# Re-timing the helper work of the first attention layer: weight rounding, block values, softmax sums and a bias broadcast

## The chip, the core and the metric

One core of a Trainium2 chip runs the whole program. The metric is device time in microseconds of one execution. The kernel before takes 1959.18 us (median of three runs, 1958.71 to 1961.47). Its five engines are named as in the profile: PE is TensorE (matmuls and transposes), DVE is VectorE, ACT is ScalarE, POOL is GpSimd, SP is SyncE, which here only issues DMAs. Each engine works through its own instructions in order and waits on semaphores.

## The reference, cut to what matters

The program is four layers in a row over x of 4 x 1024 tokens by 256. The change lies in the first one, a gated cross-attention to a context of 77 tokens with 16 heads of width 16:

```python
def _L0_xattn_ref(q, k, v, wq, bq, wk, bk, wv, bv, wo, bo):
    qh = (q @ wq.T + bq) ...            # 16 heads of 16
    kh = (k @ wk.T + bk) ...
    vh = (v @ wv.T + bv) ...
    attn = softmax(einsum('bhqd,bhkd->bhqk', qh * SCALE, kh))
    out = einsum('bhqk,bhkd->bhqd', attn, vh)
    return out @ wo.T + bo
x = x + tanh(g_xattn[0]) * _L0_xattn_ref(_layernorm(x), ctx, ctx, ...)
x = x + tanh(g_ffn[0]) * _L0_ffn_ref(_layernorm(x), ...)   # ternary weights
```

After it come a feed-forward layer, a second cross-attention and a self-attention, which the change does not touch.

## The kernel before, in words

`first_attention` treats the tokens in 32 tiles of 128, two tiles to a pair n, four pairs to a batch entry b. All engines run a loop over the same step number T from -12 to 34, and each engine's list of work for a step is written out by hand. In step T:

- PE does the scores of tile T+2, the transposes of the probabilities of tile T, in odd steps the transpose of the widened reciprocals of pair n-1 (`reciprocals`, L398) and the q projection of pair n+2, in even steps the transpose of x (`x_transpose`) and `out_proj` of pair n-2, and in every step one half of the product with the values (`pv`, L443) of pair n-1. `pv(n, 0)` waits for `o_out` of pair n-1, which `weigh` on DVE signals. `scores(T)` waits for `shift(T-1)` of DVE.
- DVE does, in even steps, `weigh` (values times reciprocals, L760), then in every step the row maximum (L752) and `shift` (L767) of tile T+2, then `recip_sum(T)` (L774, L775): the last reduction of the softmax sum and its reciprocal. Then come side jobs: `mantissas` (L799), which gathers the mantissa bits of a chunk of feed-forward weights, layer norm statistics, and in even steps the residual.
- ACT empties PSUM and does the exponential of tile T+2 (L562).
- POOL does `fold(T+2)`, three adds that shrink the 78 probabilities of each head to 10 partial sums (`half_sum` L622, `quarter` L624, `eighth` L628), then `widen(T)` (L637), which spreads the reciprocals for PE, in odd steps `add_bias` (L645), and its own side jobs: `block_v` (L657, five multiplies, once per batch entry), `round_chunk` (L650, a CAST of a weight chunk), and every eighth step `root` (L607 to L609, L95 to L98), a chain of 15 small instructions for the layer norm of the next batch entry; `offset` follows one step later.

The numbers behind the sums: `recip_sum(T)` waits until `fold(T)` is done, and `widen(T)` waits until `recip_sum(T)` is done. POOL runs `fold(T+2)` in step T. So in the kernel before DVE asks in step T for a fold that POOL did in step T-2.

22 chunks of feed-forward weights (128 x 1024 each) pass through four staging buffers. `CHUNK_STEPS` (L22) gives the step of each; POOL rounds it and DVE collects its mantissa bits in that step. SP loads chunk i after chunk i-4 was treated by both. After the loop the layer ends when the last pair is stored, and the feed-forward layer starts behind a barrier.

At the start POOL builds masks, waits for `root_done`, and enters the loop. In step -3 it waits for two small loads (`s_wide`: the value bias and the output bias) and spreads the value bias over 128 columns (`vb_wide`, L701), from which PE computes the product of the value bias with the output weights in step -1 (`v_bias`); DVE finishes it in step 0 (`whole_bias`).

Of the kernel before, what the change touches and what calls it, by code (L numbers as in the profile page):

```python
# [8 lines left out]
ALU = mybir.AluOpType  # L9
ACT = mybir.ActivationFunctionType  # L10
AX = mybir.AxisListType

P = 128
# [5 lines left out]
RSQRT_MAGIC = 0x5F3759DF  # L19
WCH = 1024  # L20
STAGE = 4
CHUNK_STEPS = (-5, -4, 1, 2, 3, 4, 5, 6, 9, 10, 11, 12, 13, 14, 18, 19, 20, 21, 22, 26, 27, 28)  # L22
MANTISSA = 0x7FFFFF


# [39 lines left out]
def spread(ap, dim, n):  # L65

    shape = list(ap.shape)
    shape[dim] = n
    return ap.broadcast_to(shape)
# [31 lines left out]
def first_attention(nc, ident, gates, gates_src, x_src, x_dst, ctxT, wqT, wkT, wvT, woT, bias, H, ffn, head, w_stage, tag):  # L101

    B, _, S = ctxT.shape
# [15 lines left out]
    RS = 4  # L119
# [25 lines left out]
    with semaphores(nc, tag) as sem, ExitStack() as ctx:  # L145
        def sb(name, shape, dt=F32):
            return ctx.enter_context(nc.sbuf_tensor(f"{tag}_{name}", shape, dt))
# [9 lines left out]
        kbias = sb("kbias", [P, C])  # L157
        kb_masked = sb("kb_masked", [P, C, HR])
        vbias = sb("vbias", [P, C])
        vb_wide = sb("vb_wide", [P, C, P])  # L160
        obias = sb("obias", [P, D])
        kt = sb("kt", [P, 2, C, HR, S])
# [14 lines left out]
        prob_all = sb("prob", [P, PR, KC * P])  # L177
        half_sum = sb("half_sum", [P, H, HALF])
        quarter = sb("quarter", [P, H, HALF // 2])
        eighth = sb("eighth", [P, 3, H, HALF // 4])  # L180
        negmax = sb("negmax", [P, H])
        rsum = sb("rsum", [P, RS, H])
        r_wide = sb("r_wide", [P, RS, H, dh])
# [45 lines left out]
        def _(sp):  # L229
# [63 lines left out]
            store_v(0)  # L293
            for i in range(2, STAGE):
                load_chunk(i)
            for dst, src in ((vbias[:, :], bv),
                             (obias[:, :], spread(bo.rearrange("(a n) -> a n", a=1), 0, P))):
                sp.dma_start(dst, src).then_inc(s_wide, 16)
            load_w(3, wo, woT)
            load_x(PB + 2)  # L300
            load_x(PB + 3)
# [298 lines left out]
        def _(pool):  # L600
# [17 lines left out]
            def fold(T):  # L618
                pool.wait_ge(a_exp, T + 1)
                if T:  # L620
                    pool.wait_ge(p_eighth, T)
                own.step(pool.tensor_tensor(half_sum[:, :, 0:S2 // 2], prob[:, T % PR, :, 0:S2 // 2],  # L622
                                            prob[:, T % PR, :, S2 // 2:S2], ALU.add))
                own.step(pool.tensor_tensor(quarter[:, :, :], half_sum[:, :, 0:HALF // 2],  # L624
                                            half_sum[:, :, HALF // 2:HALF], ALU.add))
                if T >= 3:
                    pool.wait_ge(d_r, T - 2)
                pool.tensor_tensor(eighth[:, T % 3, :, :], quarter[:, :, 0:HALF // 4],  # L628
                                   quarter[:, :, HALF // 4:HALF // 2], ALU.add).then_inc(p_eighth, 1)

            def widen(T):
# [20 lines left out]
            def block_v(b):  # L652
                pool.wait_ge(v_in, 32 * (b + 1))
                if b >= 2:
                    pool.wait_ge(e_pv, PB * (b - 1))
                for i, k, n in runs:
                    ins = pool.tensor_tensor(v_blk[:, b % 2, i:i + n, :, :], spread(v_k[:, k:k + n, :].unsqueeze(2), 2, HR),  # L657
                                             spread(v_mask[:, i:i + n, :].unsqueeze(3), 3, dh), ALU.mult)
                ins.then_inc(v_placed, 1)
# [16 lines left out]
            for i, (_, m, k) in enumerate(tiles):  # L676
                own.link(pool.affine_select(out=v_mask[:, i, :], in_=v_mask[:, i, :], compare_op=ALU.is_ge, fill=0.0,
                                            base=S - 1 - P * k + SEG * m, pattern=[[S2, HR]], channel_multiplier=-1))
            own.wait()
            pool.wait_ge(s_pad, 1)  # L680
            pool.wait_ge(root_done, 1)
            for T in STEPS:
                n, odd = divmod(T, 2)
                if T % 8 == 0 and 1 <= (T + 8) // 8 <= B:
                    root((T + 8) // 8)
                if T % 8 == 1 and 1 <= (T + 8) // 8 <= B:
                    offset((T + 8) // 8)
                if 0 <= T + 2 < TILES:
                    fold(T + 2)
                if 0 <= T < TILES:  # L690
                    widen(T)
                if odd and 0 <= n < NP:
                    add_bias(n)
                if (T + 2) % 8 == 0 and 0 <= (T + 2) // 8 < B:
                    block_v((T + 2) // 8)
                if T in CHUNK_AT:
                    round_chunk(CHUNK_AT[T])
                if T == -3:
                    pool.wait_ge(s_wide, 32)
                    for c in range(C):  # L700
                        ins = pool.tensor_copy(vb_wide[:, c, :], spread(vbias[:, c:c + 1], 1, P))  # L701
                    ins.then_inc(s_vb, 1)

        @block.vector
        def _(dve):
# [64 lines left out]
            def recip_sum(T):  # L770
                dve.wait_ge(p_eighth, T + 1)
                if T >= RS:
                    dve.wait_ge(p_wide, T - RS + 1)
                own.step(dve.tensor_reduce(rsum[:, T % RS, :], eighth[:, T % 3, :, :], AX.X, ALU.add))  # L774
                dve.reciprocal(rsum[:, T % RS, :], rsum[:, T % RS, :]).then_inc(d_r, 1)  # L775

            def whole_bias():
# [46 lines left out]
            for T in STEPS:  # L824
                n, odd = divmod(T, 2)
                if not odd and 0 <= n - 2 < NP:
                    weigh(n - 2)
                if 0 <= T + 2 < TILES:
                    row_max(T + 2)
                if 0 <= T + 2 < TILES:  # L830
                    shift(T + 2)
                if T == 0:
                    whole_bias()
                if 0 <= T < TILES:
                    recip_sum(T)
                if T in CHUNK_AT:
                    mantissas(CHUNK_AT[T])
                if T == CHUNK_STEPS[-1] + 1:
                    mantissa_found()
                b, p = divmod(T + 12, 8)  # L840
                if p < PB and 0 <= PB * b + p < NP + HEAD:
                    ln_stats(PB * b + p)
                if not odd and 0 <= n - 2 < NP:
                    residual(n - 2)
                if T == TILES:
                    judge()
# [1906 lines left out]
def laid_out(inputs):  # L2753

    import numpy as np

    def cols(v):
        return v.reshape(-1, P).T

    a = {}  # L2760
    for name, v in inputs.items():
        v = np.asarray(v)
        if name == "x":
            a[name] = v.reshape(-1, v.shape[-1])
        elif name == "ctx_1024":
            a["ctxT"] = v.transpose(0, 2, 1)
        elif name.startswith("L0_xattn_w") or (name.startswith("L0_ffn_") and name.endswith("_w")):
            a[name + "T"] = v.T
        elif name.endswith("Wkv"):
            half = v.shape[1] // 2  # L2770
            a[name[:-3] + "Wk"], a[name[:-3] + "Wv"] = v[:, :half], v[:, half:]
        elif name in ("L0_xattn_bq", "L0_xattn_bk", "L0_xattn_bv", "L1_xattn_ln_scale", "L1_xattn_ln_bias", "L0_ffn_w1_s",
                      "L0_ffn_w2_s", "L0_ffn_h1_s", "L0_ffn_h2_s"):
            a[name] = cols(v)
        else:
            a[name] = v
    return {name: np.ascontiguousarray(v) for name, v in a.items()}
# [14 lines left out]
```

## Time and profile before

| what | value |
|---|---|
| median of three runs | 1959.18 us |
| the profiled execution's own time | 1958.71 us |
| its span | 1957.0 us |
| mean granted clock | 0.985 |
| busy over the span: PE, DVE, ACT, POOL | 94%, 61%, 55%, 37% |
| the first attention layer | about 0 to 236 us of the span |

The granted clock is a share of TensorE's full speed. The shares over the whole span say little here, since the change touches only the first 236 us: there POOL is busy nearly throughout, while it has little to do in the layer behind. "Idle before" in a row is how long the engine stood before that instruction, and the name after the arrow is what ended the wait.

### The profile page before, as it was taken

What the parts mean: (1) busy time and instruction counts of PE and PEld (TensorE: products, weight loads), DVE (VectorE), ACT (ScalarE), POOL (GpSimd) and SP (SyncE); (2) the same over time, 40 slices, a digit from 0 to 9 for tenths busy, and PEclk for the clock granted to TensorE, in tenths of its full rate; (3) what the DMA queues carried; (4) which work ended last, traced back from release to release, by engine and by line L of the source; (5) the groups of instructions that cost most, each with busy time, mean ns of one, the idle gap of its engine ahead of it and who ended that gap; (6) DMA issues with size and microseconds to landing.
All of it is one profiled execution on the core that took longest, in us unless ns stands there. A gap on an engine that the chain in (4) does not pass through costs nothing. (4 is left out here: it accounts for less than half of the span.)

```text
span 1957.0 us, 60621 instructions
## 1 busy us (share of the span) xinstructions
PE 1836.1 (94%) x26589; PEld 1491.1 (76%) x26589; DVE 1190.7 (61%) x1658; ACT 1085.4 (55%) x1900; POOL 732.3 (37%) x1008
## 2 busy tenths in 40 slices
PE   6999799999999999998899988999999999999996
PEld 4666578788887888886787867788787877887875
DVE  7888533332423323242655536888988898888885
ACT  4666444443434434342545544777777777877763
POOL 6899600000010000010433322556556565656552
PEclk9999999999999999999899998999999999999999
DMA  5332100000000000010111115212332143123211
GB/s 160 101 114 69 40 10 22 1 22 1 22 12 11 22 1 22 1 66 27 53 41 33 35 39 131 73 58 62 110 96 58 57 115 96 52 68 110 75 52 35
DMA packets 147006, 106.24 MB, mean 54 GB/s; under 512 B 19993, under 2 KB 143153, under 8 KB 146737
## 3 DMA queue, kind: packets, MB, share of 16 engines
q1 hardware_dynamic: 146736, 102.28, 17.8%
q8 instruction: 215, 3.52, 0.8%
q14 instruction: 55, 0.44, 0.1%
HBM read 76.77 MB, written 25.49 MB: 52 GB/s over the span
## 5 line engine op out<-in xcount | busy, mean ns | idle before, releaser
L2251 ACT ACTIVATE E_prob<-E_ps_s,E_negmax 128x1024 f32<-128x1024 f32 x256 | 284.9, 1115 | 143.2 <-DVE E_negmax L2564 142.8
L2564 DVE TENSOR_REDUCE E_negmax<-E_ps_s 128x1 f32<-128x1024 f32 x256 | 301.5, 1219 | 82.2 <-PE E_ps_s L2070 81.8
L2571 DVE STREAM_TRANSPOSE E_prob<-E_prob 128x1024 f32<-128x1024 f32 x256 | 303.9, 1225 | 23.9 <-ACT E_prob L2251 11.5
L2089 PEld LDWEIGHTS E_ps_o<-E_prob,E_vrep 32*64 32x64 f32 x15872 | 231.5, 130 | 63.4 <-ACT head L2277 56.9
L2089 PE MATMUL E_ps_o<-E_prob,E_vrep 32*64 32x128 f32 x15872 | 262.5, 274 | 11.6 <-ACT head L2277 3.6
L1675 ACT ACTIVATE F_raw<-F_ps,ffn_scales 128x512 f32<-128x512 f32 x128 | 88.3, 690 | 287.9 <-PE F_ps L1578 287.9
L1578 PE MATMUL F_ps<-F_ha,ffn_w_rounded 128*128 128x512 f32 x1024 | 240.7, 395 | 0.0
L1578 PE MATMUL F_ps<-F_hb,ffn_w_rounded 128*128 128x512 f32 x1024 | 240.2, 395 | 0.0
L1578 PEld LDWEIGHTS F_ps<-F_ha,ffn_w_rounded 128*128 128x128 f32 x1024 | 191.1, 188 | 48.3 <-issue 1.6
L1578 PEld LDWEIGHTS F_ps<-F_hb,ffn_w_rounded 128*128 128x128 f32 x1024 | 192.1, 188 | 46.8
L2469 POOL TENSOR_TENSOR head<-head 128x512 f32<-128x512 f32 x93 | 119.3, 1283 | 248.4 <-ACT head L2277 248.4
L1766 DVE TENSOR_TENSOR F_ha<-F_raw,F_ha 128x512 fp32r<-128x512 f32 x64 | 44.3, 693 | 184.2 <-ACT F_ha L1677 184.2
L1766 DVE TENSOR_TENSOR F_hb<-F_raw,F_hb 128x512 fp32r<-128x512 f32 x64 | 44.3, 693 | 169.2 <-ACT F_hb L1677 169.2
L95 POOL TENSOR_TENSOR F_rs<-F_rs 128x4 f32<-128x4 f32 x24 | 4.8, 199 | 352.6 <-DVE F_rs L1725 351.3
L1578 PE MATMUL F_ps<-F_xt_part,ffn_w_rounded 128*128 128x512 f32 x512 | 123.8, 400 | 8.2 <-DVE F_raw L1756 4.2
L2070 PE MATMUL E_ps_s<-E_k_hi,E_q_hi 64*128 64x512 f32 x512 | 114.5, 442 | 15.0 <-ACT E_prob L2251 13.4
L1578 PEld LDWEIGHTS F_ps<-F_xt_part,ffn_w_rounded 128*128 128x128 f32 x512 | 94.1, 190 | 35.7 <-DVE F_raw L1756 9.0
L1696 POOL TENSOR_TENSOR F_xt_part<-F_xt,F_xt_part 128x1024 fp32r<-128x1024 f32 x7 | 16.9, 2409 | 252.1 <-ACT F_xt_part L1637 144.1
L2070 PE MATMUL E_ps_s<-E_k_hi,E_q_lo 64*128 64x512 f32 x512 | 102.3, 392 | 0.0
L2070 PE MATMUL E_ps_s<-E_k_lo,E_q_hi 64*128 64x512 f32 x512 | 101.3, 390 | 0.0
L2070 PEld LDWEIGHTS E_ps_s<-E_k_hi,E_q_hi 64*128 64x128 f32 x512 | 48.0, 184 | 42.6 <-ACT E_prob L2251 23.4
L1756 DVE SCALAR_TENSOR_TENSOR F_raw<-F_ps,ffn_scales,F_silu 128x512 f32<-128x512 f32 x64 | 47.7, 750 | 53.8 <-ACT F_silu L1659 53.8
(318 smaller groups left out, 3913.3 us busy)
## 6 DMA issues: line engine op xcount, KB each, us to landing
E_vrep<-E_v_all SPq DMA_DIRECT2D x128, 256.0 KB, 3.1
shared<-in_L_ffn_h_wT SPq DMA_DIRECT2D x16, 512.0 KB, 3.9
E_v_all<-E_vst SPq DMA_DIRECT2D x32, 256.0 KB, 2.3
C_x<-x SPq DMA_DIRECT2D x20, 256.0 KB, 4.2
F_x<-x SPq DMA_DIRECT2D x9, 512.0 KB, 3.7
A_x<-in_x SPq DMA_DIRECT2D x16, 256.0 KB, 5.1
x<-A_x SPq DMA_DIRECT2D x16, 256.0 KB, 2.2
x<-F_x SPq DMA_DIRECT2D x16, 256.0 KB, 2.1
```

The source lines that it names most:

```text
L95: own.step(eng.tensor_tensor(t, y, y, ALU.mult))
L1578: mm = pe.matmul(out, fw.chunk(w, name, k, j * P, (j + 1) * P), a[:, k, :], start=k == 0 and i == 0, stop=k == K - 1 and i == len(parts) - 1)
L1675: act.activation(raw[:, u % 2, :], ps[:, u % 4, :], ACT.Gelu, scale=scale).then_inc(u_raw, 1)
L1696: pool.tensor_tensor(xt_part[1][:, :, :], xt[:, :, :], xt_part[0][:, :, :], ALU.subtract).then_inc(xt_lo, 1)
L1756: dve.scalar_tensor_tensor(out=dst, in0=ps[:, 2 * (j % 2) + 1, :], scalar=scales[:, 1, j:j + 1], in1=silu[:, j % 2, :], op0=ALU.mult, op1= ...
L1766: dve.tensor_tensor(dst, raw[:, u % 2, :], hi, ALU.subtract).then_inc(u_lo, 1)
L2070: mm = pe.matmul(ps_s[:, j, keys], a[rows, c % 2, cols], k[rows, c % 2, keys], start=i == 0, stop=i == 2)
L2089: mm = pe.matmul(low[64 * j:64 * j + 64, g, :], vrep[rows, slot, KB // 4 * (quarter % 2) + k, dh * j:dh * (j + 1)], prob[rows, u % 2, :, j ...
L2251: act.activation(prob[:, s // UT % 2, s % UT, j, :], ps_s[:, j, :], ACT.Exp, bias=negmax[:, at:at + 1], scale=1.0, accum_out=den[:, 2 * c ...
L2469: pool.tensor_tensor(part[:, 0, :], part[:, 0, :], part[:, 1, :], ALU.add).then_inc(part_added, 1)
L2564: dve.tensor_reduce(negmax[:, at:at + 1], ps_s[:, j, :], AX.X, ALU.max, negate=True).then_inc(d_max, 1)
L2571: dve.transpose(at, at).then_inc(d_t, 1)
```

## The change: what it does

Five edits, all in the first attention layer.

1. `CHUNK_STEPS` gets other numbers: two chunks move ahead of step 0 (to -2 and -1), and the others are spread to steps that reach to 27. Before: -5, -4, 1 to 6, 9 to 14, 18 to 22, 26 to 28.
2. `block_v` moves one step later, from steps 6, 14, 22 (and -2) to steps 7, 15, 23 (and -1).
3. DVE calls `recip_sum(T+1)` in step T and not `recip_sum(T)`; `eighth` has two buffers and not three.
4. The value bias is loaded as 256 single numbers from a plain vector (before: 128 runs of two numbers that lay side by side), is spread by a multiply with a tile of ones, and this is done ahead of POOL's loop: the wait for `s_wide` stands in front of everything that POOL does in the loop.
5. `whole_bias` moves on DVE from step 0 to the end of step -1.

```diff
-CHUNK_STEPS = (-5, -4, 1, 2, 3, 4, 5, 6, 9, 10, 11, 12, 13, 14, 18, 19, 20, 21, 22, 26, 27, 28)
+CHUNK_STEPS = (-5, -4, -2, -1, 1, 3, 4, 5, 6, 7, 9, 11, 12, 13, 15, 17, 19, 20, 21, 23, 25, 27)
...
-        eighth = sb("eighth", [P, 3, H, HALF // 4])
+        eighth = sb("eighth", [P, 2, H, HALF // 4])
...
-            for dst, src in ((vbias[:, :], bv),
+            for dst, src in ((vbias[:, :], bv.rearrange("(c p) -> p c", p=P)),
                              (obias[:, :], spread(bo.rearrange("(a n) -> a n", a=1), 0, P))):
-                sp.dma_start(dst, src).then_inc(s_wide, 16)
+                sp.dma_start(dst, src, allow_slow_non_contiguous=True).then_inc(s_wide, 16)
...
-                if T >= 3:
-                    pool.wait_ge(d_r, T - 2)
-                pool.tensor_tensor(eighth[:, T % 3, :, :], quarter[:, :, 0:HALF // 4],
+                if T >= 2:
+                    pool.wait_ge(d_r, T - 1)
+                pool.tensor_tensor(eighth[:, T % 2, :, :], quarter[:, :, 0:HALF // 4],
...
             own.wait()
+            own.step(pool.memset(ones[:, :], 1.0))
+            pool.wait_ge(s_wide, 32)
+            for c in range(C):
+                ins = pool.tensor_tensor(vb_wide[:, c, :], ones[:, :], spread(vbias[:, c:c + 1], 1, P), ALU.mult)
+            ins.then_inc(s_vb, 1)
             pool.wait_ge(s_pad, 1)
             pool.wait_ge(root_done, 1)
             for T in STEPS:
...
-                if (T + 2) % 8 == 0 and 0 <= (T + 2) // 8 < B:
-                    block_v((T + 2) // 8)
+                if (T + 1) % 8 == 0 and 0 <= (T + 1) // 8 < B:
+                    block_v((T + 1) // 8)
                 if T in CHUNK_AT:
                     round_chunk(CHUNK_AT[T])
-                if T == -3:
-                    pool.wait_ge(s_wide, 32)
-                    for c in range(C):
-                        ins = pool.tensor_copy(vb_wide[:, c, :], spread(vbias[:, c:c + 1], 1, P))
-                    ins.then_inc(s_vb, 1)
...
-                own.step(dve.tensor_reduce(rsum[:, T % RS, :], eighth[:, T % 3, :, :], AX.X, ALU.add))
+                own.step(dve.tensor_reduce(rsum[:, T % RS, :], eighth[:, T % 2, :, :], AX.X, ALU.add))
...
-                if T == 0:
-                    whole_bias()
-                if 0 <= T < TILES:
-                    recip_sum(T)
+                if 0 <= T + 1 < TILES:
+                    recip_sum(T + 1)
...
+                if T == -1:
+                    whole_bias()
```

Where it moves instructions. On POOL between steps 6 and 8 of the kernel before, ahead of the second `root` (which begins with L607, A_rs from A_mv); A_v_blk is `block_v`, the CAST is `round_chunk`, A_half_sum to A_eighth is one fold, A_r_wide is `widen`, A_x is `add_bias`:

```order
L657 TENSOR_TENSOR A_v_blk<-A_v_k,A_v_mask 128x96
L657 TENSOR_TENSOR A_v_blk<-A_v_k,A_v_mask 128x32
L650 CAST ffn_w_rounded<-shared 128x1024
L622 TENSOR_TENSOR A_half_sum<-A_prob 128x16x39
L624 TENSOR_TENSOR A_quarter<-A_half_sum 128x320
L628 TENSOR_TENSOR A_eighth<-A_quarter 128x160
L637 COPY A_r_wide<-A_rsum 128x128 x2
L645 TENSOR_TENSOR A_x<-A_x,A_obias 128x512
L607 TENSOR_SCALAR A_rs<-A_mv 128x8
```

The same place on POOL in the changed kernel, whose line numbers are one higher:

```order
L651 CAST ffn_w_rounded<-shared 128x1024
L623 TENSOR_TENSOR A_half_sum<-A_prob 128x16x39
L625 TENSOR_TENSOR A_quarter<-A_half_sum 128x320
L629 TENSOR_TENSOR A_eighth<-A_quarter 128x160
L638 COPY A_r_wide<-A_rsum 128x128 x2
L646 TENSOR_TENSOR A_x<-A_x,A_obias 128x512
L658 TENSOR_TENSOR A_v_blk<-A_v_k,A_v_mask 128x160
L658 TENSOR_TENSOR A_v_blk<-A_v_k,A_v_mask 128x96
L658 TENSOR_TENSOR A_v_blk<-A_v_k,A_v_mask 128x160
L658 TENSOR_TENSOR A_v_blk<-A_v_k,A_v_mask 128x96
L658 TENSOR_TENSOR A_v_blk<-A_v_k,A_v_mask 128x32
L651 CAST ffn_w_rounded<-shared 128x1024
```

`block_v` stood ahead of the fold of tile 9 and stands behind it now, and a second CAST stands between that fold and the `root`.

On DVE at the end of step 9 and the start of step 10 the names alone don't show what moved, since `recip_sum` reads alike for every tile. In the changed kernel:

```order
L753 TENSOR_REDUCE A_negmax<-A_ps_s 128x16
L768 TENSOR_TENSOR A_prob<-A_ps_s,A_negmax 128x16x77
L775 TENSOR_REDUCE A_rsum<-A_eighth 128x16
L776 RECIPROCAL A_rsum<-A_rsum 128x16
L800 TENSOR_TENSOR A_w_bits<-A_w_bits,shared 128x1024
L761 TENSOR_TENSOR A_o<-A_ps_o,A_r_t 128x512
```

The rows are those of before, but the reduction of A_eighth is that of tile 10 and not of tile 9, and behind it in the queue stand the mantissas (A_w_bits) and `weigh` (A_o) of pair 3.

## Rows read from the trace of the kernel before

**Rows 1.** Busy time by stretch: us, busy (instructions), then granted clock, DMA share, GB/s
```profile
30.00:232.00 202.00, 183.92 (x1718) 130.23 (x1717) 161.76 (x219) 126.09 (x229) 177.93 (x276) 0.97 0.25 73
```
**Rows 2.** Same view, PE alone, around four waits
```profile
45.00:56.00 11.00, 8.47 (x47) 0.69 0.16 49
99.00:107.00 8.00, 5.76 (x36) 0.79 0.35 116
150.00:158.00 8.00, 6.35 (x62) 1.00 0.10 33
```
**Rows 3.** Timeline of PE at the second root: start us, us, instruction, idle before
```profile
94.46 1.50 PE L443 MATMUL A_ps_o<-A_pt,A_v_blk 128*32 128x256 f32 x18
...
101.44 0.79 PE L398 MATMUL A_ps_m<-ident,A_r_wide 128*128 128x128 f32 x4 [2.23 <-POOL A_r_wide L637]
```
**Rows 4.** Timeline of POOL, 80 to 101 us
```profile
80.37 1.70 POOL L657 TENSOR_TENSOR A_v_blk<-A_v_k,A_v_mask 128x160 f32<-128x160 f32 x5
82.01 1.04 POOL L650 CAST ffn_w_rounded<-shared 128x1024 fp32r<-128x1024 f32 x1
...
87.83 0.24 POOL L607 TENSOR_SCALAR A_rs<-A_mv 128x8 f32<-128x8 f32 x1
...
90.82 1.01 POOL L98 TENSOR_TENSOR A_rs<-A_rs 128x8 f32<-128x8 f32 x1
...
92.79 0.20 POOL L98 TENSOR_TENSOR A_rs<-A_rs 128x8 f32<-128x8 f32 x1
...
95.64 0.49 POOL L628 TENSOR_TENSOR A_eighth<-A_quarter 128x160 f32<-128x160 f32 x1
...
100.86 0.53 POOL L637 COPY A_r_wide<-A_rsum 128x128 f32<-128x128 f32 x2
```
**Rows 5.** Timeline of ACT: the exponential of tile 9
```profile
80.36 1.23 ACT L562 ACTIVATE A_prob<-A_prob 128x1232 f32<-128x1232 f32 x1
```
**Rows 6.** Timeline of DVE, steps 9 and 10
```profile
90.10 0.31 DVE L774 TENSOR_REDUCE A_rsum<-A_eighth 128x16 f32<-128x160 f32 x1
...
90.61 1.16 DVE L799 TENSOR_TENSOR A_w_bits<-A_w_bits,shared 128x1024 int32<-128x1024 int32 x1
92.08 0.69 DVE L760 TENSOR_TENSOR A_o<-A_ps_o,A_r_t 128x512 f32<-128x512 f32 x1 [0.31 <-PE A_ps_o L443]
92.82 1.44 DVE L752 TENSOR_REDUCE A_negmax<-A_ps_s 128x16 f32<-128x1232 f32 x1
94.30 1.44 DVE L767 TENSOR_TENSOR A_prob<-A_ps_s,A_negmax 128x1232 f32<-128x1232 f32 x1
```
**Rows 7.** Timeline of PE at the first, third and fourth root
```profile
44.05 0.81 PE L412 MATMUL A_ps_s<-A_kt,A_q 32*128 32x154 f32 x16
...
47.97 1.12 PE L398 MATMUL A_ps_m<-ident,A_r_wide 128*128 128x128 f32 x4 [2.53 <-POOL A_r_wide L637]
...
146.61 1.50 PE L443 MATMUL A_ps_o<-A_pt,A_v_blk 128*32 128x256 f32 x18
...
152.86 0.66 PE L398 MATMUL A_ps_m<-ident,A_r_wide 128*128 128x128 f32 x4 [1.50 <-POOL A_r_wide L637]
...
197.20 1.50 PE L443 MATMUL A_ps_o<-A_pt,A_v_blk 128*32 128x256 f32 x18
...
202.73 0.66 PE L398 MATMUL A_ps_m<-ident,A_r_wide 128*128 128x128 f32 x4 [0.78 <-POOL A_r_wide L637]
```
**Rows 8.** Timeline of POOL: last fold instruction behind the first, third, fourth root
```profile
42.15 0.49 POOL L628 TENSOR_TENSOR A_eighth<-A_quarter 128x160 f32<-128x160 f32 x1
...
146.89 0.49 POOL L628 TENSOR_TENSOR A_eighth<-A_quarter 128x160 f32<-128x160 f32 x1
...
196.90 0.49 POOL L628 TENSOR_TENSOR A_eighth<-A_quarter 128x160 f32<-128x160 f32 x1
```
**Rows 9.** Timeline of POOL at the start
```profile
21.80 0.53 POOL L701 COPY A_vb_wide<-A_vbias 128x128 f32<-128x128 f32 x2 [2.37 <-DMA A_obias<-in_L_xattn_bo]
24.98 1.51 POOL L622 TENSOR_TENSOR A_half_sum<-A_prob 128x624 f32<-128x624 f32 x1 [2.64 <-ACT A_prob L562]
```

More of the change, by code:

```diff
@@ L159, in first_attention @@
         vbias = sb("vbias", [P, C])
+        ones = sb("ones", [P, P])
         vb_wide = sb("vb_wide", [P, C, P])
@@ L2771, in laid_out @@
             a[name[:-3] + "Wk"], a[name[:-3] + "Wv"] = v[:, :half], v[:, half:]
-        elif name in ("L0_xattn_bq", "L0_xattn_bk", "L0_xattn_bv", "L1_xattn_ln_scale", "L1_xattn_ln_bias", "L0_ffn_w1_s",
+        elif name in ("L0_xattn_bq", "L0_xattn_bk", "L1_xattn_ln_scale", "L1_xattn_ln_bias", "L0_ffn_w1_s",
                       "L0_ffn_w2_s", "L0_ffn_h1_s", "L0_ffn_h2_s"):
```

## The prediction

> **What bounds the kernel now.** I first read the busy time by stretch. From 30 to 232 us, the loop of the first attention layer, POOL is busy 177.93 of 202 us, PE 183.92, DVE 161.76 [rows 1]. Three engines run near their limit, so a wait on one soon becomes a wait on another. Then I read the timeline of PE. The two-tile period is dense, except at four places, all the same: PE stands at the transpose of the widened reciprocals and is released by POOL, for 2.53, 2.23, 1.50 and 0.78 us, 7.0 us together [rows 3, 7]. They come in steps 3, 11, 19 and 27, three steps behind a `root`. The POOL timeline gives the reason. At the second root POOL starts the chain of small instructions at 87.83, ends it at 92.99, ends the fold of tile 10 at 96.13 and starts the `widen` for which PE waits at 100.86 [rows 4]. POOL never stands still in between. These waits also cost clock: the granted clock is 0.69 and 0.79 of full speed in the stretches around the first two and 1.00 around the third [rows 2]. Of 11 and 8 us that is 3.4 and 1.7 us of full-speed time.
>
> So the layer is PE's pace plus four hold-ups by POOL, one behind each root. Of each edit I ask what it does there.
>
> **Edit 2 and 1, POOL ahead of a root.** Before, the order is `block_v`, CAST, fold of tile 9, `widen`, `add_bias`, root. Now one CAST, fold, `widen`, `add_bias`, `block_v`, CAST, root. The 1.70 us of `block_v` and one CAST of 1.04 us [rows 4] now lie behind the fold: 2.74 us more between fold and root. The fold can't move ahead by as much. The CAST ahead of it ended at 83.05, and the exponential it needs at 81.59 [rows 4, 5]: at most 1.46 us is gained. So the root starts about 1.3 us later. I take 1.3 us for roots 2, 3 and 4 (bounds 0, if the fold moves by all of it, and 2.74 us, if it doesn't move). Ahead of the first root the folds wait for their exponentials, as that of tile 0 did for 2.64 us [rows 9], so no fold can move ahead there, and `block_v` leaves a place where POOL had time to spare: there I take the full 2.74 us.
>
> **Edit 3, the reciprocal sum one step early.** This is the large term. Nothing waits for `recip_sum`: no hold-up of PE or POOL ends on it. What the edit adds is a wait. In step 9 DVE now asks for the fold of tile 10, which POOL runs in step 8 behind the root. DVE comes to this place at 90.10 [rows 6]; the fold ends at 96.13 [rows 4], with the 1.3 us at 97.4. DVE stands about 7 us. Behind it in the queue are the reciprocal, the mantissas, `weigh` of pair 3, the row maximum and the shift of tile 12. `weigh` is what `pv(4, 0)` on PE waits for, and that wait is new.
>
> The sum for the second root: 97.4, plus 0.1 for the signal, plus 0.51 (from 90.10 to 90.61) for reduction and reciprocal, plus 1.16 for the mantissas and 0.69 for `weigh` [rows 6]: 99.9 us. `pv` started at 94.46 before [rows 3], so PE is held 5.4 us. From `pv` to the transpose of the reciprocals PE took 4.75 us (94.46 to 99.21, which is 101.44 less the wait of 2.23) [rows 3]. It arrives there at 104.6; POOL has the `widen` ready at 100.86 + 0.53 + 1.3 = 102.7 [rows 4], so the old wait is gone, but PE is 3.2 us later than its 101.44. The new wait takes the place of the old one and is longer.
>
> Third root: the fold ends at 146.89 + 0.49 + 1.3 = 148.7 [rows 8], plus the same 2.5 us (in step 17 there is now a chunk too) gives 151.2 for `pv`, 4.6 us after 146.61. PE was ready at the transpose at 151.36; now 155.9, against 152.86: 3.1 us [rows 7]. Fourth root: 196.90 + 0.49 + 1.3 + 2.5 = 201.2, 4.0 us after 197.20; ready at 201.95 + 4.0 = 205.9, against 202.73: 3.2 us [rows 7, 8].
>
> First root: the fold of tile 2 ends at 42.64 + 2.74 = 45.4 [rows 8]. DVE goes on with 0.1 + 0.51 + 1.16 us, then the row maximum and shift of tile 4 at 1.44 us each [rows 6]: 50.0. The scores of tile 5 wait for that shift and started at 44.05 before: 6.0 us of wait. PE was ready for the transpose at 45.44, now at 51.4, against 47.97: 3.5 us [rows 7].
>
> Together 3.5 + 3.2 + 3.1 + 3.2 = 13.0 us. The clock: idles of 2.53 and 2.23 us were followed by the lower clock, that of 1.50 was not [rows 2, 3, 7]. By those rows the third and fourth root now pay it too, with idles of 4 to 4.6 us. I take 1.7 us each, the smaller of the two prices in rows 2 (bounds 0 and 3.4): 3.4 us. The lower clock at roots 1 and 2 stays as it is.
>
> **What the moved chunks give.** Two chunks leave the loop behind step 0: two CASTs of 1.04 us and two mantissa instructions. Those drop out at steps where POOL later waits for an exponential, so PE gains nothing: 0. Bound: the two CASTs and one further us each on POOL, 4 us. That further us is seen in the trace: the mantissa instruction runs on DVE from 90.61, and a POOL instruction of 128x8 issued at 90.82 took 1.01 us where its like at 92.79 took 0.20 [rows 4, 6]. The Trainium skill says why (SBUF — State Buffer, section Who interferes with whom): a DVE instruction with two SBUF inputs shares a port with a POOL instruction that reads SBUF, and the later one waits. The trace agrees. By that rule alone the change would be a gain, with fewer such meetings in the loop; it is the rival "relief" below.
>
> **Edit 4, the start.** POOL waits for both bias loads at the front of the loop. Before, it rounded two chunks and then waited 2.37 us, until 21.80 [rows 9]. Now the chunks come after: 21.80 + 0.53 + two CASTs of 1.04 = 24.4. The first fold waits for an exponential and started at 24.98: hidden. If each meets a mantissa instruction and takes 1 us more, some 1.5 us shows. What stands behind: SP holds chunk 4 until chunk 0 is rounded, and behind chunk 4 in its queue are the loads of the values that `block_v` needs. Both CASTs had ended by 19.43 before (21.80 less the wait) and end at 24.4 now, so these loads come 5 us later; `block_v` itself comes later too, behind one more fold. I take 0, bound 4 us. The Trainium skill (DMA: Bandwidth & Descriptors, section Why small descriptors are slow) would have the load of 256 single numbers slower; the wait ended on the other load, that of the output bias [rows 9], so it changes nothing here until it lands behind that.
>
> **Edit 5** moves two short DVE instructions that PE needs only for the first `pv` from one step to the end of the step before: 0.
>
> **Sum.** 1958.71 us of the profiled execution + 13.0 + 3.4 = 1975.1 us. That execution lies 0.5 us under the median of 1959.18. I predict 1975.
>
> **The rivals.**
> - *Held by the late root alone* (slower, smaller). DVE has room to catch up, so its wait doesn't reach PE, and only the later start of the roots is paid: 2.7 + 3 x 1.3 = 6.6 us, 1965 us. For it: DVE is the least busy of the three, 161.76 of 202 us [rows 1]. Against: `weigh` lies directly behind the wait and `pv` needs it at once. It decides if `weigh` is ready within 2 us of PE's coming.
> - *Relief* (faster). The chunks, not the roots, made POOL late. If fewer meetings per period bring each `widen` ahead of PE, the 7.0 us of waits and the 5.1 us of clock go: 1947 us at best; with only the two chunks of POOL work saved, 4 us, 1955. It decides from the point at which the folds behind a root end before DVE asks, some 6 us earlier than in rows 4 and 6. Nothing in the rows moves them by so much.
> - *Late start.* The sum above, and in addition the values come late for `block_v`: up to 4 us more, 1979.
> - *No effect*: the waits move, and PE's own work fills the time; 1957 to 1961. Against it: PE does nothing while it waits in order.
>
> **How the numbers follow.** Forecast 0.66, late root alone 0.13, late start 0.06, no effect 0.08, relief 0.07. A measurement of this kernel tells 0.2%, 3.9 us, from no change. Slower: 0.66 + 0.13 + 0.06 less 0.01 for the low edge = 0.84; same 0.09; faster 0.07. The range goes down to 1963 (1.3 us per root turned to 0 takes 3.9, the clock price 3.4, a part of DVE's wait absorbed the rest), which takes in rival one, and up to 1982 (clock at 3.4 us per root adds 3.4, roots 2.74 us late add 4.3, less what overlaps). The likeliest case alone: 1969 to 1981.
>
> **What would show it.** In the changed profile: DVE waits at the reduction of A_eighth, released by POOL's `eighth`, four times for some 5 to 7 us, where the whole layer had almost none. PE waits at `pv` for DVE's A_o three times for 4 to 5 us, once at the scores for DVE's A_prob, and its wait for A_r_wide is gone. The granted clock drops below 1.00 behind all four roots. The feed-forward layer starts some 16 us later, and all behind it is as long as before. I am wrong if the wait of DVE is short or absent, if POOL's root starts no later against PE, or if PE's waits in the loop add up to no more than before.

## The result and the profile after

| what | before | after |
|---|---|---|
| median of the timed runs, us | 1960.33 (1958.71 to 1961.95, 4 runs) | 1981.03 (1979.26 to 1983.30, 4 runs) |
| the profiled execution's own time, us | 1958.71 | 1977.79 |
| its span, us, and mean granted clock | 1957.0, 0.985 | 1976.1, 0.981 |
| first layer, until the feed-forward layer's first transpose | 241.5 us | 253.8 us |
| the rest of the span | 1715.5 us | 1722.3 us |

The ratio is 1.0101 [1.0082, 1.012]: slower by 1%. A later comparison of the same two kernels gave 1.0086 [1.007, 1.0101], 1976.94 against 1961.16 us. The profiled execution and one more of the kernel after took 1977.79 and 1975.92 us. By the two ratios the change costs some 17 to 20 us (the medians differ by 20.7 and 15.8). Of the 19.1 us between the two profiled spans, 12.3 lie in the first layer and 6.8 behind it, where not one instruction differs; the last experiment asks which of them the change caused.

The first view is the list of waits between 30 and 255 us of the kernel after: who waits for whom, then us in total, how many times, the longest. Here, too, the line numbers of the kernel after are one higher than those of the kernel before.

```profile
DVE A_rsum L775 <- POOL A_eighth L629: 29.7, 13, 6.4
POOL A_half_sum L623 <- ACT A_prob L563: 28.1, 14, 3.2
...
PE A_ps_o L444 <- issue: 13.0, 3, 4.4
...
PE A_ps_s L413 <- DVE A_prob L768: 5.5, 2, 4.9
...
PE A_ps_m L399 <- POOL A_r_wide L638: 0.5, 1, 0.5
```

The same view of the kernel before, from the same stretch:

```profile
POOL A_half_sum L622 <- ACT A_prob L562: 9.4, 6, 3.2
...
PE A_ps_m L398 <- POOL A_r_wide L637: 7.0, 4, 2.5
...
DVE A_rsum L774 <- POOL A_eighth L628: 0.4, 1, 0.4
```

PE's 7.0 us behind the widened reciprocals are down to 0.5. In their place stand 13.0 us in three waits at `pv` and 4.9 at the scores, and DVE waits 29.7 us for POOL's fold where it waited 0.4; 22.2 us of them are four waits, one behind each root. POOL itself stands idle for longer than before, 28.1 us against 9.4, and still every root holds PE up: what counts is when POOL is late, not how busy it is.

PE in the kernel after (start us, duration us, engine, instruction, idle before), at the second root, where it answers to [rows 3], and at the third and fourth:

```profile
99.43 2.76 PE L444 MATMUL A_ps_o<-A_pt,A_v_blk 128*32 128x256 f32 x18 [4.22 <-issue]
...
105.65 0.60 PE L399 MATMUL A_ps_m<-ident,A_r_wide 128*128 128x128 f32 x4
...
153.82 2.55 PE L444 MATMUL A_ps_o<-A_pt,A_v_blk 128*32 128x256 f32 x18 [4.42 <-issue]
...
208.19 2.31 PE L444 MATMUL A_ps_o<-A_pt,A_v_blk 128*32 128x256 f32 x18 [4.40 <-issue]
```

The transpose of the reciprocals no longer waits, but comes at 105.65 and not at 101.44. The idle time stands at `pv`, all three times, and the profile calls its end "issue": it found no releaser. DVE's rows name it. The first four are those of the start, for later; the others are the second root and answer to [rows 6]:

```profile
28.68 1.50 DVE L800 TENSOR_TENSOR A_w_bits<-A_w_bits,shared 128x1024 int32<-128x1024 int32 x1
...
31.44 0.40 DVE L782 TENSOR_TENSOR A_obias<-A_ps_o,A_obias 128x256 f32<-128x256 f32 x1
31.87 0.78 DVE L783 TENSOR_SCALAR A_obias<-A_obias,gates 128x256 f32<-128x256 f32 x1
...
34.03 1.44 DVE L768 TENSOR_TENSOR A_prob<-A_ps_s,A_negmax 128x1232 f32<-128x1232 f32 x1
...
89.39 1.44 DVE L768 TENSOR_TENSOR A_prob<-A_ps_s,A_negmax 128x1232 f32<-128x1232 f32 x1
97.05 0.32 DVE L775 TENSOR_REDUCE A_rsum<-A_eighth 128x16 f32<-128x160 f32 x1 [6.21 <-POOL A_eighth L629]
...
97.57 1.16 DVE L800 TENSOR_TENSOR A_w_bits<-A_w_bits,shared 128x1024 int32<-128x1024 int32 x1
98.65 0.68 DVE L761 TENSOR_TENSOR A_o<-A_ps_o,A_r_t 128x512 f32<-128x512 f32 x1
```

`weigh` ends at 99.33 and `pv` starts at 99.43. It waits in the code for just that. POOL, which answers to [rows 4]:

```profile
82.13 1.52 POOL L623 TENSOR_TENSOR A_half_sum<-A_prob 128x624 f32<-128x624 f32 x1 [1.57 <-ACT A_prob L563]
...
86.82 1.69 POOL L658 TENSOR_TENSOR A_v_blk<-A_v_k,A_v_mask 128x160 f32<-128x160 f32 x5
88.45 1.04 POOL L651 CAST ffn_w_rounded<-shared 128x1024 fp32r<-128x1024 f32 x1
89.58 0.24 POOL L608 TENSOR_SCALAR A_rs<-A_mv 128x8 f32<-128x8 f32 x1
...
96.53 0.48 POOL L629 TENSOR_TENSOR A_eighth<-A_quarter 128x160 f32<-128x160 f32 x1
```

The root starts 1.75 us later, at 89.58 instead of 87.83, but the fold that DVE waits for ends only 0.88 us later, at 97.01 instead of 96.13. The root itself got shorter: its slow instruction of 1.01 us in [rows 4] met the mantissas on DVE. Now DVE stands still while the root runs, its mantissas come at 97.57, and every instruction of the root takes 0.20 to 0.25 us.

PE's clock, in the columns of [rows 2]: behind the wait at the scores, at the first root, and in the stretches ahead of the third and fourth reciprocal transposes.

```profile
34.00:42.00 8.00, 6.38 (x34) 0.57 0.20 68
45.00:56.00 11.00, 9.79 (x95) 1.00 0.14 49
...
153.00:161.00 8.00, 7.18 (x55) 0.79 0.06 18
208.00:216.00 8.00, 7.74 (x57) 0.79 0.11 35
```

Last, the layer cut at the four transposes of the reciprocals behind a root: stretch, its length, PE's busy time (instructions), granted clock, DMA share, GB/s. Before:

```profile
0.00:47.97 47.97, 29.83 (x204) 0.99 0.54 163
47.97:101.44 53.47, 50.20 (x452) 0.94 0.34 101
101.44:152.86 51.42, 49.10 (x453) 0.97 0.34 104
152.86:202.73 49.87, 47.65 (x453) 1.00 0.22 64
202.73:241.50 38.77, 28.07 (x254) 0.96 0.10 33
```

After:

```profile
0.00:49.11 49.11, 29.70 (x205) 0.90 0.60 181
49.11:105.65 56.54, 49.42 (x454) 0.97 0.31 87
105.65:160.04 54.39, 49.14 (x454) 0.97 0.31 93
160.04:214.41 54.37, 49.14 (x454) 0.97 0.18 53
214.41:253.80 39.39, 28.11 (x256) 0.99 0.10 34
```

The five lengths grow by 1.1, 3.1, 3.0, 4.5 and 0.6 us. In the fourth row, length less busy time is PE's idle time, 2.22 us before and 5.23 after, and the clock goes from 1.00 to 0.97, which is 1.6 us of 54.37: 3.0 + 1.6 = 4.6 us, against the measured 4.5.

The first length, 1.1 us, understates the change. The two executions did not enter the loop at the same time: PE starts the scores of tile 2 at 30.37 us before and at 28.14 after, and kernels with the same code up to there start them anywhere from 28.3 to 30.4 us (before, once more, e1, e7, e9). Counted from the scores of tile 2, the first length is 17.60 us before and 20.97 after, so it grows by 3.4 us, and the whole layer by 14.5. Of these, 11.1 are idle time of PE and 3.4 are busy time, which is what the lower clock makes of the same work.

### The profile page after: what moved, and what is told of

It is laid out like the page before. It is cut to its first block and busy times, and to the rows that moved or that the text cites. A ratio compares the mean times of both kernels' runs of the same rounds, so it can differ in the third digit from the quotient of the medians.

```text
span 1976.1 us, 60623 instructions
## 1 busy us (share of the span) xinstructions
PE 1841.2 (93%) x26589; PEld 1493.8 (76%) x26589; DVE 1188.5 (60%) x1658; ACT 1083.7 (55%) x1900; POOL 723.0 (37%) x1009
```

## The experiments

Each kernel was profiled, and timed beside the kernel before on the same chip. "Layer" is the time until the feed-forward layer's first transpose in the profiled execution (before 241.5, after 253.8).

**The reciprocal sum alone, and all but it.** `e1_recip_only` is the kernel before with edit 3 alone:

```diff
-                if 0 <= T < TILES:
-                    recip_sum(T)
+                if 0 <= T + 1 < TILES:
+                    recip_sum(T + 1)
```

> The kernel before with edit 3 alone: the reciprocal sum of tile T+1 in step T, and two eighth buffers. Theory (DVE is held by the fold behind the root): at the second root the fold ends at 96.1 as before, then 0.1 + 0.51 + 1.16 + 0.69 us, pv at 98.6 instead of 94.46, the transpose of the reciprocals at 103.3 instead of 101.44; third and fourth root without a chunk behind the wait, 0.6 us each; first root 0.7 us. Together some 4 us, 6 with a lower clock after two of the waits; DVE waits for eighth about 5 us behind each root. Rival (only the late root costs, DVE's wait is absorbed): 0 us, because the root starts where it did.

Measured: 1969.25 us, ratio 1.0043 [1.003, 1.0055], 8.4 us; layer 245.7. `e2_all_but_recip` is the kernel after with that one edit undone (the value bias spread by a copy, with no tile of ones).

> The changed kernel with edit 3 undone: recip_sum(T) in step T and three eighth buffers. The value bias is spread by a copy as in the kernel before, still at the front of the loop, since the tile of ones has no room beside the third buffer. Theory: DVE's long waits and PE's waits at pv go, PE waits again for the widened reciprocals, a little longer than before, since the roots start 1.3 us late: 3 to 6 us over the kernel before, 14 to 17 us under the changed one. Rival (late root or chunks are the main cost): at least 12 us over the kernel before.

Measured: 1965.9 us, ratio 1.003 [1.0018, 1.0042], 5.9 us; layer 244.3. The two halves, 8.4 and 5.9, make 14.3 of the change's 17 to 20 us: they nearly add up. DVE at the second root in `e1_recip_only`:

```profile
92.36 0.32 DVE L774 TENSOR_REDUCE A_rsum<-A_eighth 128x16 f32<-128x160 f32 x1 [3.86 <-POOL A_eighth L628]
...
93.96 0.68 DVE L760 TENSOR_TENSOR A_o<-A_ps_o,A_r_t 128x512 f32<-128x512 f32 x1
```

and PE there:

```profile
94.74 1.50 PE L443 MATMUL A_ps_o<-A_pt,A_v_blk 128*32 128x256 f32 x18 [1.89 <-issue]
...
100.71 0.63 PE L398 MATMUL A_ps_m<-ident,A_r_wide 128*128 128x128 f32 x4 [1.23 <-DVE A_x L788]
```

The wait is edit 3's: it is there with none of the rest. But at the second root it is 3.86 us and not 6.21, and `pv` is held 1.89 us and not 4.22. The other 2.3 us come with the late root. The 8.4 us are more than the 4 to 6 expected. A term that nobody had counted is DVE's residual: PE waits for it 9.0 us in nine waits, against 1.8 us in three before. In `e2_all_but_recip` DVE waits 6.5 us for the fold and not 29.7, and PE's old wait is longer than in [rows 3]:

```profile
100.69 0.66 PE L398 MATMUL A_ps_m<-ident,A_r_wide 128*128 128x128 f32 x4 [3.41 <-POOL A_r_wide L637]
```

Its four such waits sum to 9.5 us (7.0 before). So each half of the change costs by itself, and both do so behind the same roots.

**The later block values alone.** `e3_blockv_only`, the kernel before with edit 2:

```diff
-                if (T + 2) % 8 == 0 and 0 <= (T + 2) // 8 < B:
-                    block_v((T + 2) // 8)
+                if (T + 1) % 8 == 0 and 0 <= (T + 1) // 8 < B:
+                    block_v((T + 1) // 8)
```

> The kernel before with edit 2 alone: block_v one step later. Theory: the 1.70 us of block_v stand between fold and root, of which up to 1.4 us come back, since the fold ahead can start earlier: 0.3 to 1.7 us per root in PE's wait for the widened reciprocals, 1 to 5 us in all. Rival (block_v's place does not matter): 0 us.

Measured: 1970.43 us (1959.96 to 1976.95), ratio 1.0044 [1.0011, 1.0076]; layer 246.8. The interval is wide, from 2 to 15 us; that it costs something is shown, how much is not. PE's four waits for A_r_wide sum to 9.9 us, 2.9 more than before. Behind the third, of 1.71 us, the granted clock is 0.79 from 154 to 162 us, where [rows 2] have 1.00 behind a wait of 1.50. So in this execution the late root cost clock beside its wait; whether the longer wait brought it stays open, as the last section shows.

**The chunks alone.** `e4_chunks_only`, the kernel before with edit 1:

```diff
-CHUNK_STEPS = (-5, -4, 1, 2, 3, 4, 5, 6, 9, 10, 11, 12, 13, 14, 18, 19, 20, 21, 22, 26, 27, 28)
+CHUNK_STEPS = (-5, -4, -2, -1, 1, 3, 4, 5, 6, 7, 9, 11, 12, 13, 15, 17, 19, 20, 21, 23, 25, 27)
```

> The kernel before with edit 1 alone: the new steps of the chunks. Theory: a CAST of 1.04 us comes right in front of the roots 2 to 4, and one behind the fold of tile 1: about 1 us per root later, 2 to 4 us slower in all. Rival (relief, fewer meetings of mantissas and POOL instructions in the loop): 4 us faster.

Measured: 1964.65 us, ratio 1.0021 [1.001, 1.0032]; layer 241.8. The waits for A_r_wide are 3.43 us at the first root and 3.38 at the second, and the four sum to 10.1 us, 3.1 more than before. That is as expected: two chunks fewer in the loop did not help, and the chunks at steps 7, 15 and 23, between fold and root, are the likely cost. `e8_before_new_chunks` asked for the gain alone: one chunk leaves the loop to step -2, others leave steps 5, 14 and 21 for 25 and 29, and none is put in front of a root:

```diff
-CHUNK_STEPS = (-5, -4, 1, 2, 3, 4, 5, 6, 9, 10, 11, 12, 13, 14, 18, 19, 20, 21, 22, 26, 27, 28)
+CHUNK_STEPS = (-5, -4, -2, 1, 2, 3, 4, 6, 9, 10, 11, 12, 13, 18, 19, 20, 22, 25, 26, 27, 28, 29)
```

> The kernel before with other chunk steps, chosen so that fewer CASTs lie between POOL's last wait for an exponential and the widen behind a root: (-5, -4, -2, 1, 2, 3, 4, 6, 9, 10, 11, 12, 13, 18, 19, 20, 22, 25, 26, 27, 28, 29); the chunks of steps 5, 14 and 21 are taken out. Theory: PE's waits behind roots 2 to 4 of 2.23, 1.50 and 0.78 us shrink by about 1 us each, and the lower clock behind the second goes: 3 to 6 us faster than before. Rival (the number of chunks in the loop matters, not their place): 1 us or nothing.

Measured: 1961.77 us, ratio 1.0006 [0.9995, 1.0018]. No gain, no loss, where 3 to 6 us had been expected. The wait at the second root fell only from 2.23 to 1.51 us, at the first it stayed at 2.54, at the fourth it rose from 0.78 to 1.51, and a new one of 2.10 us came near the end of the loop. The five waits sum to 8.1 us, against 7.0: other chunk steps moved the waits and did not shorten their sum.

**The bias alone.** `e5_bias_only`, the kernel before with edit 4 (the loads as single numbers, the wait ahead of the loop, the spread by a copy):

```diff
-            for dst, src in ((vbias[:, :], bv),
+            for dst, src in ((vbias[:, :], bv.rearrange("(c p) -> p c", p=P)),
...
+            pool.wait_ge(s_wide, 32)
+            for c in range(C):
+                ins = pool.tensor_copy(vb_wide[:, c, :], spread(vbias[:, c:c + 1], 1, P))
+            ins.then_inc(s_vb, 1)
...
-                if T == -3:
-                    pool.wait_ge(s_wide, 32)
```

> The kernel before with edit 4 alone (bias loaded as single numbers, spread at the front of POOL's loop; by a copy, since the tile of ones has no room). Theory: hidden by the exponential of tile 0, 0 us, at most 1. Rival (late start: the queue of SP behind the first CAST brings the values late for block_v): up to 4 us slower.

Measured: 1959.8 us, ratio 0.9991 [0.9978, 1.0005]: nothing. POOL's rows at the start:

```profile
22.56 0.53 POOL L682 COPY A_vb_wide<-A_vbias 128x128 f32<-128x128 f32 x2 [15.45 <-DMA A_obias<-in_L_xattn_bo]
...
25.02 1.50 POOL L622 TENSOR_TENSOR A_half_sum<-A_prob 128x624 f32<-128x624 f32 x1
```

POOL stands for 15.45 us, and its first fold starts at 25.02, where [rows 9] have 24.98. The wait still ends on the load of the output bias, not on that of the 256 single numbers, so what these cost does not show.

**A shorter root.** If the roots are what holds everything up, a shorter root must give time back in both kernels. These two leave out two of the three Newton steps of the `root` inside the loop, 8 of its 15 instructions:

```diff
-                newton(own, pool, half, y, t)
+                newton(own, pool, half, y, t, 1)
```

> The changed kernel with one Newton step instead of three in POOL's root (two thirds of the iteration left out, for the layer norms of batch entries 1 to 3 and the two pairs behind them). One Newton step takes 1.17 us on POOL (90.49 to 91.67 in the changed kernel), so each root is 2.3 us shorter. Theory: DVE's wait of 6.2 to 6.4 us behind each root and PE's wait of 4.2 to 4.4 us at pv shrink by 2.3 us each, and the lower clock behind them shrinks or goes: 7 to 12 us faster than the changed kernel. Rival (the roots are not what holds DVE): less than 2 us.

> The kernel before with the same short root. Theory: PE's four waits for the widened reciprocals, 7.0 us, shrink by up to 2.3 us each and nearly go, 6.8 us, and with them most of the 5.1 us of lower clock: 6 to 11 us faster than before. Rival (PE's own work fills the time): 0 us.

Measured: on the kernel after 1966.1 us, 1.0024 [1.0007, 1.004] of before; layer 241.8, 12.0 us less than after. On the kernel before 1950.53 us, 0.9949 [0.9932, 0.9966], which is 10 us faster; layer 229.4, 12.1 us less. The prediction had put down 7.0 us of waits and 5.1 of clock for the roots, together just these 12.1; but against the second profile of before, with its layer of 238.7 us, the gain is 9.3. So it is 9 to 12 us, and the roots hold both kernels up. Both gain alike: with the short root the change still costs 12 to 15 us. PE at the second root in `e7_before_short_root` has neither the wait nor the low clock that followed it in [rows 2]:

```profile
93.44 0.66 PE L398 MATMUL A_ps_m<-ident,A_r_wide 128*128 128x128 f32 x4
...
94.88 1.96 PE L383 MATMUL A_ps_m<-A_xt,A_wq 128*128 128x256 f32 x8
```

In `e6_after_short_root` PE stands at `pv` for 1.93, 2.11 and 2.11 us, in place of 4.22, 4.42 and 4.40:

```profile
95.33 1.50 PE L444 MATMUL A_ps_o<-A_pt,A_v_blk 128*32 128x256 f32 x18 [1.93 <-issue]
```

**The root on another engine.** The same question without leaving anything out: `e9_before_root_on_dve` (and `e10_after_root_on_dve`) take `root` and `offset` from POOL's loop and let DVE do them ahead of its residual:

```diff
-                if T % 8 == 0 and 1 <= (T + 8) // 8 <= B:
-                    root((T + 8) // 8)
-                if T % 8 == 1 and 1 <= (T + 8) // 8 <= B:
-                    offset((T + 8) // 8)
...
+                if T % 8 == 0 and 1 <= (T + 8) // 8 <= B:
+                    b = (T + 8) // 8
+                    dve.wait_ge(stat, b)
+                    whole_root(mv[:, b % 2, :, :], rs[:, b % 2, :, :]).then_inc(root_done, 1)
```

> The kernel before with the roots of batch entries 1 to 4 computed by DVE (the chain it already runs for entry 0, 2.5 us from 13.51 to 15.97) behind the mantissas of steps 0, 8, 16 and 24, and none on POOL. At those steps 8, 16 and 24 DVE stood 1.67 us waiting for the out projection. Theory (POOL's root is what makes the widen late): PE's four waits of 7.0 us go, and 5 us of lower clock with them, less about 1 us per root for a later residual: 8 to 12 us faster than before. Rival (the work only moves to DVE, which is as full): 0 us, or slower.

> The changed kernel with the same move of the roots to DVE. Theory (the edits cost time only because the root stands in front of the fold that DVE now asks for early): DVE's waits of over 6 us for eighth and PE's waits of over 4 us at pv go, and the time comes to within 4 us of the kernel before with this move: 25 us or more under the changed kernel. Rival (the edits cost something of their own): it stays 8 us or more above the kernel before with this move.

Measured: 1969.97 us, 1.0056 [1.0038, 1.0074], on the kernel before; 1976.82 us, 1.0087 [1.0069, 1.0106], on the kernel after. What was expected of POOL came: the waits for A_r_wide are gone, and POOL stands idle 35.8 us in `e9_before_root_on_dve`. The time did not follow, since DVE became late instead. DVE at the second root there:

```profile
84.65 1.20 DVE L710 TENSOR_TENSOR A_rs<-A_rs 128x8 f32<-128x8 f32 x1
85.89 1.43 DVE L711 TENSOR_TENSOR A_rs<-A_rs 128x8 f32<-128x8 f32 x1
87.35 0.17 DVE L712 SCALAR_TENSOR_TENSOR A_rs<-A_rs 128x8 f32<-128x8 f32 x1
...
89.62 0.75 DVE L784 SCALAR_TENSOR_TENSOR A_x<-A_ps_m,gates,A_x 128x512 f32<-128x512 f32 x1
```

and PE:

```profile
90.52 1.09 PE L398 MATMUL A_ps_m<-ident,A_r_wide 128*128 128x128 f32 x4 [3.37 <-DVE A_x L784]
```

The chain took 5.5 us (84.10 to 89.62), and PE waits for the residual behind it. The 8 to 12 us faster that had been expected did not come; the rival, that the work only moves to DVE, did. The experiment shows that POOL's lateness and PE's old wait hang together. It does not show what a free root would be worth; the short root comes nearer to that.

The second of the two comes out level with the kernel after, where 25 us less had been expected, and 6 to 7 us above the first, between what the theory allowed (4) and what the rival said (8). With no root on POOL, DVE's waits for the fold sum to 9.0 us and not to 29.7, and PE no longer stands at `pv` for 4 us. By this, most of what the five edits cost, 17 to 20 us, hangs on the root in front of the fold. But DVE is late here for a reason of its own, so the 6 to 7 us are no clean measure of the rest.

**The rest of the program.** `c2_after_again` and `c1_before_again` are the two kernels once more, unchanged.

> The changed kernel once more, beside the kernel before on the same chip. In the profiled executions the first layer accounts for 12.3 us of 19.1 and the layers behind it for 6.8 us, though their instructions are the same. Theory A (the rest is the difference of single executions in TensorE's clock): the first layer is again 12 us longer than before, the rest differs by another amount, and the medians differ by less than 19 us. Theory B (the layers behind really get slower): 19 to 21 us again.

> The kernel before once more, for a second profile. Theory A: the time from the start of the feed-forward layer to the end, 1715.5 us in the first profile, is some us longer in this one, without any cause in the code. Theory B: it is 1715.5 within 1 us.

Measured: 1976.94 us (6 runs) for the kernel after, layer 255.3, rest 1720.4. For the kernel before one execution of 1963.42 us, layer 238.7, rest 1723.0. So theory A holds. The rest of the span in all profiled executions, where all fourteen run the same code: before 1715.5, after 1722.3, and in the order of the experiments (e1 to e10) 1717.6, 1719.9, 1725.5, 1724.0, 1718.3, 1722.9, 1717.5, 1720.8, 1718.1, 1719.0. The kernel before holds both the lowest value and, once more, one above that of after. So the 6.8 us behind the layer are scatter between executions. The layer is longer by 12.3 us in the first pair of profiles, by 16.6 in the second. Counted from the scores of tile 2 it is 14.5 and 17.8.

The second profile of before holds a surprise. PE waits at the first two roots as in [rows 3, 7], even a little longer, but the granted clock behind both waits stays at 1.00, where [rows 2] have 0.69 and 0.79:

```profile
47.06 0.66 PE L398 MATMUL A_ps_m<-ident,A_r_wide 128*128 128x128 f32 x4 [2.81 <-POOL A_r_wide L637]
...
98.31 0.66 PE L398 MATMUL A_ps_m<-ident,A_r_wide 128*128 128x128 f32 x4 [2.53 <-POOL A_r_wide L637]
```

```profile
45.00:56.00 11.00, 7.98 (x70) 1.00 0.17 54
98.00:106.00 8.00, 7.54 (x66) 1.00 0.23 74
```

## Why the prediction was right, step by step

- *What bounds the kernel*: right in the waits. A shorter root takes 9 to 12 us out of the layer of before, where waits and clock were put at 7.0 + 5.1. The clock is the weak half of this: the same waits came without the 5.1 us in the second profile of before. The view by stretch had said only that three engines are nearly full; the four waits in PE's timeline said where.
- *Edit 3, the wait added*: right in place and size for roots two to four. DVE's waits at the four roots were 3.22, 6.21, 6.39 and 6.37 us (about 7 forecast for the second), and `pv` was held 4.22, 4.42 and 4.40 (5.4, 4.6, 4.0). The term 3.2 + 3.1 + 3.2 is one of waits; PE's idle time grew by 3.9, 2.9 and 3.0 us in these three stretches, and by 3.4, 2.6 and 3.1 in the second pair of profiles.
- *First root*: the size came, by another path. It was put at 3.5 us; counted from the scores of tile 2 the stretch grew by 3.4 us, and by 3.7 in the second pair. But the working had PE held for 6.0 us at the scores of tile 5, behind DVE's long wait. DVE's wait for the fold was only 3.22 us, and these scores waited 0.66. PE was held 4.88 us two tiles earlier, at the scores of tile 3, where it had waited 1.34 before. Its idle time in the stretch grew by 0.8 us, as its old waits went; the other 2.6 us are slower work, at a clock of 0.57 from 34 to 42 us. That the sum fits is luck. Why DVE was late at tile 3: in its rows at the start the mantissas of a moved chunk (28.68, 1.50 us) and `whole_bias` (31.44 to 32.65; edit 5) lie ahead of the row maximum and of the shift that PE waits for (34.03), though PE had done the scores of tile 2 at 28.95. The kernels with edit 5 wait 3.9 to 5.5 us at those scores (after, once more, e2, e6, e10), the nine profiles without it 1.3 to 1.4. All with edit 5 have edits 1, 2 and 4 too, and edits 1, 2 and 4 one by one leave the wait at 1.35. So edit 5, put at 0, was perhaps not free, alone or together with edit 1; its own two instructions take 1.2 us. No run has it alone, and its share stays open.
- *The late root*: forecast 1.3 us, 1.75 seen at the second (87.83 to 89.58). The fold ahead of it started 0.9 us sooner. Of the 1.75 us only 0.88 reached the fold behind the root, since the root no longer meets the mantissas: here the rival "relief" had a true part, of 0.8 us. The rival that charged the late roots alone said 6.6 us. `e2_all_but_recip`, which is nearly that case, cost 5.9, of which the waits for A_r_wide are 2.5 and the longer wait at the scores of tile 3 is 2.8.
- *Clock*: right in size in the first pair, for a reason that does not hold. Between 30 and 232 us the full-speed time lost (one less the granted clock, added up over windows of 2 us) rose from 5.1 to 8.5 us, by the 3.4 forecast. The two prices of 1.7 us at the third and fourth root came: 0.79 over 8 us. At the second root the price stayed. At the first it moved: 1.00 from 45 to 56 us, where [rows 2] have 0.69, and 0.57 from 34 to 42 us instead. At the 1.2 GHz level `pv` at the second root took 2.76 us, at 2.4 GHz 1.50. In the second pair the same sum rose from 1.7 to 12.0 us. So "the lower clock at roots 1 and 2 stays as it is" and the fixed 1.7 us per root were lucky: the clock behind like waits differs from execution to execution.
- *Moved chunks and start*: 0 forecast for both. Edit 4 by itself cost nothing. Edit 1 cost 4.1 us by itself where it had been counted only as part of the late root.
- *The sum*: 13.0 + 3.4 = 16.4 us. Counted from the scores of tile 2, the layer grew by 11.1 us of idle and 3.4 of busy time in the first pair, by 11.9 and 5.9 in the second: 14.5 and 17.8. The medians differ by 17 to 20 us by their ratios, and 1975 lies 2 to 6 us under the two medians of after. Part of that distance is not the change: the profiled execution of before, on which the sum was built, had the shortest rest of all fourteen, 1715.5 us, where their mean is 1720.3. With that mean, 1.7 us around the span (1958.71 less 1957.0) and the layers of 253.8 and 255.3, after comes to 1976 to 1977 us. It was measured at 1976.94 and at 1981.03; the 4 us between these two medians are not explained, but single executions beside the second took 1975.92 and 1977.79.

## What to carry to other kernels

Before asking for a result a step earlier, look who makes it and what stands ahead of it in that engine's queue: here nobody waited for the reciprocal sum, and asking early made DVE stand behind POOL's root, its longest chain, with the work PE needed next queued behind. A wait that is taken from one engine's row is only gone if the last link, here the root on POOL, ends sooner. And build a sum for a long kernel on the stretch that changes, since the rest of this one moves by 10 us from execution to execution without any change. Take a second profile before putting a price on the clock.

## What the hardware showed beyond expectation

- Small DVE instructions are not small beside POOL. In `e9_before_root_on_dve` two 128x8 TENSOR_TENSORs took 1.20 and 1.43 us and ended at 85.85 and 87.32. POOL's instructions of that time, the addition of the bias and the first add of a fold, ended at 85.82 and 87.29. The same lines took 0.17 us in the chain at the start of the program, and there the whole chain of 13 took 2.4 us and not 5.5. The Trainium skill (SBUF — State Buffer, section Who interferes with whom) says that DVE and POOL share one port pair, held by one of them at a time. The trace agrees, and shows the size: the slow DVE instructions had two SBUF tensors as inputs and ended with POOL's, while those of one tensor ahead of them took 0.11 to 0.29 us. The root was priced by its short durations (2.5 us) when it was moved; it cost twice that.
- The length of PE's idle did not settle whether the lower clock followed. At the roots and the scores, every wait of over 3.3 us that was looked at was followed by it. Below, it went both ways. Followed: 1.71 us in e3 (the q projection behind it took 3.65 us for eight matmuls), one of 2.11 in e6 (`pv` 2.78 us), 2.23 and 2.53 in the first profile of before. Not followed: 1.66 in e4 (1.97 us for eight matmuls), the other of 2.11 in e6 (`pv` 1.50 us), 1.71, 2.53 and 2.81 in the second profile of before, and 2.87 at the fourth root in e2 (1.00 from 206 to 214 us). So the same late root can cost 1.7 us and more, or nothing, which may be a part of why the edits don't add up exactly.
